# Last stage of a fused decoder kernel: ScalarE writes the dense layer's bias into PSUM in place of a bias matmul

## The reference

```python
x = input.reshape(-1, shape[-1])          # LayerNorm of the 2048 tokens
dots = softmax(x @ centroids.T / 0.1)     # 64 clusters
hits = dots > 0.01
query_sel = any(hits, axis=1); cluster_sel = any(hits, axis=0)
row_sel = cluster_sel[assignments]
dense = x @ weight.T + bias               # 512 x 512
out = where(query_sel[:, None] & row_sel[None, :], dense, 0)
# and then: x = x + out
```

## Time and profile before

| | |
|---|---|
| median of 3 runs | 1656.03 us (1653.91 to 1657.03) |
| profiled execution, its own time | 1652.99 us |
| span of its profile | 1651.3 us, 29775 instructions |
| mean granted TensorE clock | 0.967 of full speed |
| last stage, first transpose to last `dense_out` | 1569.85 to 1635.62 us of the span |

### The profile page before, as it was taken

One profiled execution on the slowest core, in us unless ns is written; L12 is line 12 of the kernel. 1 busy time (PEld: TensorE's weight loads), 2 busy tenths in 40 slices (PEclk: granted clock), 3 DMA queues, 4 the chain that ended last, 5 costly groups with the idle time before them and its releaser, 6 DMA issues. The chain is left out here.

```text
span 1651.3 us, 29775 instructions
## 1 busy us (share of the span) xinstructions
PE 1499.1 (91%) x11322; PEld 796.1 (48%) x11323; DVE 1237.5 (75%) x2276; ACT 825.6 (50%) x1752; POOL 267.0 (16%) x247
## 2 busy tenths in 40 slices
PE   5799999999999999999999987799999988777695
PEld 4455455555555555555555553344444444344253
DVE  6567667668667667667767787799888885999777
ACT  3343433424324334243342332777888864888652
POOL 2001102002001011011011000001111103889620
PEclk7799999999999999999999998899999999999898
DMA  7032231321312313222221122122222350867502
GB/s 267 1 78 52 62 93 27 78 77 30 95 57 52 91 43 73 65 54 63 66 63 52 26 103 100 40 45 46 45 44 54 67 99 1 149 105 119 77 1 102
DMA packets 274121, 114.06 MB, mean 69 GB/s; under 512 B 239184, under 2 KB 255696, under 8 KB 273744
## 3 DMA queue, kind: packets, MB, share of 16 engines
q1 hardware_dynamic: 235104, 79.26, 22.2%
q10 hardware_dynamic: 38896, 33.03, 6.5%
HBM read 45.15 MB, written 11.53 MB: 34 GB/s over the span
## 5 line engine op out<-in xcount | busy, mean ns | idle before, releaser
L576 PE MATMUL pj<-XT,WQ 128*128 128x512 f16 x1536 | 338.9, 381 | 6.5 <-PEq L370 6.5
L618 PE MATMUL xp<-WO,OT 128*128 128x512 f16 x1536 | 340.5, 381 | 2.7 <-DVE X L815 2.7
L618 PEld LDWEIGHTS xp<-WO,OT 128*128 128x128 f16 x1536 | 148.3, 98 | 185.9 <-issue 14.9
L576 PEld LDWEIGHTS pj<-XT,WQ 128*128 128x128 f16 x1536 | 148.7, 98 | 182.1 <-DVE WKV L285 6.8
L696 ACT ACTIVATE E<-E 128x512 f32<-128x512 f32 x64 | 40.3, 629 | 328.1 <-DVE E L792 328.1
L815 DVE SCALAR_TENSOR_TENSOR X<-xp,X 128x512 f32<-128x512 f32 x128 | 88.4, 691 | 118.1 <-PE xp L618 117.1
L1019 PE MATMUL db<-W0T,XD 128*128 128x448 f16 x768 | 156.1, 362 | 16.5 <-DVE XD L1217 11.0
L556 POOL TENSOR_TENSOR VW<-VW,XB 128x1024 f32<-128x1024 f32 x14 | 33.0, 2357 | 770.4 <-DVE VW L98 770.4
L1037 PE MATMUL eb<-W1T,DT 128*128 128x512 f16 x672 | 147.7, 379 | 4.3 <-DMA DT<-HL 2.1
L757 DVE SCALAR_TENSOR_TENSOR QT<-pj,QT 128x512 f16<-128x512 f32 x128 | 88.1, 688 | 69.7 <-ACT QT L679 69.7
L1019 PEld LDWEIGHTS db<-W0T,XD 128*128 128x128 f16 x768 | 75.6, 100 | 94.8 <-DVE XD L1217 12.0
(11 more groups left out here) (228 smaller groups left out, 2388.7 us busy)
## 6 DMA issues: line engine op xcount, KB each, us to landing
W0T<-in_L_xattn_wq ACTq DMA_DIRECT2D x7, 1024.0 KB, 5.3
W0T<-in_L_xattn_wo ACTq DMA_DIRECT2D x7, 1024.0 KB, 5.1
CS<-in_ctx SPq DMA_DIRECT2D x4, 1024.0 KB, 10.0
X<-in_x SPq DMA_DIRECT2D x4, 1024.0 KB, 11.2
out<-X SPq DMA_DIRECT2D x8, 512.0 KB, 3.6
XB<-in_L_ffn_W ACTq DMA_DIRECT2D x28, 128.0 KB, 2.8
w0t<-XB ACTq DMA_DIRECT2D x7, 512.0 KB, 3.3
w1t<-W0T ACTq DMA_DIRECT2D x7, 512.0 KB, 3.8
```

The lines of the kernel that those rows point to most:

```text
L576: last = pe.matmul(bank[:, :], w, src[:, b, k, tokens], start=n == 0, stop=n == 3 * KC - 1)
L618: last = pe.matmul(xp[i % 2][:, :], OT[:, a, j, i * P:(i + 1) * P], WO[:, b, j, :], start=n == 0, stop=n == 3 * REP - 1)
```

## The change

From the third tile on (pairs 1 to 7) the bias matmul is gone. ScalarE has a new step, `seed(p, r)`: it waits until VectorE has emptied the bank `dn[r]` of the tile two before (`dn_out`), writes 64 times the bias into the bank, and increments `seeded`. TensorE's wait on `dn_out` ahead of the `lg` matmuls is gone, and ahead of the `dn` matmuls it waits for `seeded`; those matmuls then add onto what is in the bank. Tiles 0 and 1 keep the bias matmul. There are 14 bias matmuls less and 14 ScalarE instructions more.

```diff
@@ ffn1, TensorE
             def products(p, r):
                 pe.wait_ge(S["tp_lo"], p * 2 + (r + 1))
                 if not (isinstance(p, int) and p == 0):
-                    pe.wait_ge(S["dn_out"], p * 2 + (r - 1))
                     pe.wait_ge(S["exp_done"], p * 2 + (r - 1))
...
                 last.then_inc(S["lg_done"], 1)
-                pe.matmul(dn[r][:, :], rows[:, :], BS[:, :], start=True, stop=False)
+                if isinstance(p, int) and p == 0:
+                    pe.matmul(dn[r][:, :], rows[:, :], BS[:, :], start=True, stop=False)
+                else:
+                    pe.wait_ge(S["seeded"], p * 2 + (r - 1))
                 for n, (k, (a, b)) in enumerate([(k, ab) for k in range(KC) for ab in PASSES]):
-                    last = pe.matmul(dn[r][:, :], XT[:, r, a, k, :], WT[:, b, k, :], start=False, stop=n == 3 * KC - 1)
+                    last = pe.matmul(dn[r][:, :], XT[:, r, a, k, :], WT[:, b, k, :], start=False, stop=n == 3 * KC - 1,
+                                     skip_group_check=not (isinstance(p, int) and p == 0))
@@ ffn1, ScalarE
+            def seed(p, r):
+                act.wait_ge(S["dn_out"], p * 2 + (r - 1))
+                act.activation(dn[r][:, :], BI[:, :], ACT.Copy, scale=WEIGHT_SCALE).then_inc(S["seeded"], 1)
+
...
                 high(p, 0)
                 exps(p - 1, 1)
+                seed(p, 0)
                 high(p, 1)
                 exps(p, 0)
+                seed(p, 1)
                 if live(p + AHEAD):
                     stats_scalar(act, 3, (p + AHEAD,))
```

More of the change, by code:

```diff
@@ L466, in fused_decoder_kernel @@
         ffn0_scope.close()
-        ffn1(nc, sb, pb, sem, X, ident, rstd, nmr, (ln_moments, ln_scales) + ln[1:], last_weights, out)
+        ffn1(nc, sb, pb, sem, X, ident, rstd, nmr, (ln_moments, ln_scales) + ln[1:], last_weights, BI, out)
 def attention0(nc, sb, pb, sem, X, ident, XT, CT, w0, w1, w0t_dram, w1t_dram, ahead_of_ffn0,
@@ L1825, in _, with ffn1 @@
             early_statistics(1)
-def ffn1(nc, sb, pb, sem, X, ident, rstd, nmr, ln, last_weights, out):
+def ffn1(nc, sb, pb, sem, X, ident, rstd, nmr, ln, last_weights, BI, out):
     AHEAD = 2
@@ L1847, in ffn1 @@
         names = ("xn_done tp_done tp_hi tp_lo dn_done lg_done dn_out "
-                 "max_done nmax_done exp_done limit_done hit_done any_done qs_done count_done csel_done  x_done stored")
+                 "max_done nmax_done exp_done limit_done hit_done any_done qs_done count_done csel_done seeded x_done stored")
         S = {n: sem(ph, "f1_" + n) for n in names.split()}
```

## The result

The changed kernel took 1662.3 us (median of 6, 1659.7 to 1668.2) against 1654.4 us for the kernel before (median of 6, 1651.5 to 1657.0), a ratio of 1.0052 with a 95% interval of 1.003 to 1.0074. The forecast was 1665.1 us and +0.55%, the range 1661.8 to 1668.2.

What follows compares the result with a forecast made beforehand. The prediction took a ring of VectorE and ScalarE to bound pairs 1 to 5, TensorE only pairs 6 and 7. 8.4 us there plus 0.7 in the tail, 9.1 on 1656.0, gave 1665.1 us, range 1661.8 to 1668.2.

Steps and rivals of the forecast that it cites:

- VectorE and ScalarE set the pace in pairs 1 to 5: Steps of 8.05 us are VectorE's work plus a wait for ScalarE's root; TensorE has 0.86 us to spare.
- hole: VectorE's wait before the reciprocal for ScalarE's square root: 0.53 us before, forecast about 2.2 us after the change.
- The root queued behind `seed(p,1)`: On ScalarE, table load and root wait behind the second seed: 1.68 us more in each of five steps, 8.4 us.
- `seed(p,0)` costs nothing in pairs 1 to 5: The first seed delays ScalarE's copy, which still ends at 1589.88, ahead of `low` at 1590.16.
- The tail: Pairs 6 and 7, without statistics: 0.7 us longer with the seeds, although four bias matmuls are gone.
- the ring: Pairs 1 to 5: VectorE's step plus the root wait, 8.05 us; tail: transposes, copy, `low`, `dense_out`, seed, matmuls.
- the root's followers: `nmr`, GpSimd's normalising and the exponential's table load: all move with the late root, so are counted once.
- TensorE's pace: Rival: TensorE sets the pace, so removing the bias matmuls saves their full 2.9 us, 1653.1 us; 3 in 100.
- Seeds hidden: Rival: seeds fit into ScalarE's idle time, only the tail's four matmuls count, -0.8 us, 1655.2 us; 4 in 100.
- A drain behind a PSUM write: Rival: a pause ahead of the table load behind a seed, up to 6.4 us more, 1671.5 us; 3 in 100.
- TensorE's clock: Rival: TensorE's clock falls to 1.2 GHz, TensorE sets the pace at 13.5 us a pair, 1684 us; 2 in 100.

Runs made afterwards that it cites:

- e4: Kernel before with the bias matmul left out from the third tile on, nothing in its place: stage 56.11 us against 56.75 before, ratio 0.9999.
- e8: Kernel before with square root and table load ahead of the second exponential, ScalarE's steps written out: stage 53.78 us against 56.75 before, ratio 0.9988.
- e5: Changed kernel with GpSimd's second tile of each pair held back until VectorE's hits are done: stage 65.45 us against 66.68 changed, ratio 1.0044.
- e1: Changed kernel with the square root and its table load ahead of the second seed: stage 57.16 us against 66.68 changed, ratio to before 1.0004.
- e3: Changed kernel with only the second tile of each pair seeded, first tiles keeping bias matmul and wait: stage 66.47 us against 66.68 changed, ratio 1.0051.
- e2: Changed kernel with only the first tile of each pair seeded, second tiles keeping bias matmul and wait: stage 56.91 us against 66.68 changed, ratio 0.9988.
- e7: Changed kernel with seeds in pairs 6 and 7 alone, pairs 1 to 5 as before: tail 16.92 us against 16.51 before, ratio 1.0016.
- e6: Kernel before with square root and table load ahead of the second exponential, still looped: stage 62.68 us against 56.75 before, ratio 1.004.

## Why the prediction was right, and where it was off

- **VectorE and ScalarE set the pace in pairs 1 to 5.** Right. e4 shows it from one side (no bias matmuls, steps the same), e8 from the other (hole closed, steps 0.62 us shorter).
- **The root queued behind `seed(p,1)`, 1.68 us in each of five steps.** Right in place and size: the hole grew by 1.65 us, and e5, where GpSimd is kept away from the hits, has 48.54 us for the five steps, 8.3 more than before against 8.4 in the forecast. e1 and e3 show that it is this seed and its place. Its duration was 0.601 us, taken as 0.59, inside the bounds of the earlier trace rows.
- **`seed(p,0)` costs nothing in pairs 1 to 5.** Right: e2 has 40.26 us there.
- **The tail, +0.7 us.** Right in its sign and mis-sized: e7 measures +0.41. The forecast let ScalarE's copy begin 0.60 us behind the seed; in the profile after it begins 0.53 us behind (1627.11 to 1627.64), before the seed has ended, and takes 0.58 us and not 0.60. Each pass through the ring was therefore some 0.1 us too long in the sum, and there are three.
- **Missing from the sum: GpSimd.** The forecast had the root's followers "meet the ring at the same offsets as before". That held for the first `XN` of a pair, but not for the second. In the steps of pairs 2, 4 and 6 its buffer is free by the time the first is done, GpSimd runs both tiles together (the x2 of its row), and three hits instructions lose 0.4 us each, 1.2 us in all (shown by e5).
- **Sum.** 8.3 + 0.4 + 1.2 = 9.9 us in the stage, where 9.1 were forecast; the two misses went opposite ways. Whole executions give 0.52% of 1654.4, 8.6 us, with an interval of 5 to 12. That the median of 1662.3 us lies inside the range owes something to luck: it is 0.5 us from the lower end, and the median before came out 1.6 us below the 1656.0 that the forecast started from.
- **The rivals.** TensorE's pace: out (e4). Seeds hidden: true of the first seed alone, and in pairs 1 to 5 alone (e2, e7). A drain behind a PSUM write: the table load starts 0.02 us after the seed ends (1592.07, 1592.09), no drain shows. The profile before could have said so. The forecast holds that no table load there follows a write to PSUM, but in the stage of the first feed-forward layer one does, 0.01 us behind the end of the write to the bank `db` (1068.94 + 0.53 = 1069.47):

```profile
1068.94 0.53 ACT L1114 ACTIVATE db<-SH 128x448 f32<-128x448 bf16 x1
1069.48 1.28 ACT L1105 ACT_TABLE_LOAD   x1
```

  TensorE's clock: the forecast had it at full speed, and it fell in places; it did not set the pace (below).

## What to carry to other kernels

An engine that is idle for two fifths of the time is no free place for work: what counts is what is queued behind the new instruction while it waits, and whether the engine that it waits for will itself want that next. Here moving one line, with the same instructions, is worth 9.5 us. Before taking work off the engine that looks busiest, check who releases its waits: a start that follows another engine's end by the same 0.10 us every time is a wait, whatever the profile calls it, and leaving the work out in an experiment (e4) bounds the gain, for the order that stands, before anything is built.

## What the runs showed of the hardware that I had not expected

- A VectorE instruction on 128x64 in SBUF (HT) ran 0.65 in place of 0.25 us while GpSimd normalised a tile, and ended 0.04 to 0.06 us behind GpSimd's end; with GpSimd moved away it took 0.25 or 0.26 us everywhere (e5). The Trainium skill (SBUF — State Buffer, SBUF: two separate sides) has GpSimd and some kinds of VectorE instruction contend for a shared port pair, which the first of them locks for its whole instruction. That agrees with these rows. In the same stretch the reduction from PSUM kept its 0.21 us and a small instruction in SBUF (128x1) its 0.15 us.
- TensorE's granted clock fell to a mean of 0.62, which is partly the 1.2 GHz level, in two stretches that follow a wait of 2.29 us, and not in a third behind the same wait. The windows of the changed kernel:

```profile
1588.10:1592.60 4.50, 4.47 (x14) 1.84 (x15) 3.19 (x12) 2.02 (x5) 0.00 (x0) 0.62 0.00 0
...
1607.90:1612.50 4.60, 4.56 (x15) 2.18 (x16) 3.20 (x12) 2.11 (x5) 0.00 (x0) 0.63 0.01 2
...
1627.70:1631.00 3.30, 3.24 (x23) 1.85 (x24) 2.37 (x8) 1.17 (x5) 0.00 (x0) 1.00 0.00 0
```

  The twelve matmuls took 4.45 and 4.17 us there in place of 2.75. VectorE's ring was long enough to cover it: in e5 a block of 4.39 us stands in a step of 9.70 us, like the others. By the rows under e5 the slower blocks even spared VectorE the overlap with GpSimd in the steps behind them. Why the third one kept its clock stays open.
- A square root moved inside a loop brought a third table load in each step, of 1.28 us; written out, it was gone (e6, e8). In e6 the loop is entered with the root's table and its body ends with the exponential's, so that its head is reached with either; in the kernel before both are the root's. That this is the reason is my reading, no run tests it.
